# Moving two convolution taps from VectorE to TensorE in the last stage of a recurrent block, with a new VectorE order

## The chip, the cores and the metric

The kernel runs on one core of one Trainium2 chip. The metric is the device time of one execution in microseconds (us). Each time is the median of several executions. The profile is one of these executions, seen by the hardware profiler. All times inside it count from the start of its span.

Engine names: PE is TensorE (PEld its weight loads), DVE is VectorE, ACT is ScalarE, POOL is GpSimd, SP is SyncE.

## The reference, cut to what matters

There are 8 sequences of 512 tokens with 128 channels. Layer 0 is a causal attention multiplied by a gated top-2 mixture of experts. Layer 1, which the change touches, has a causal depthwise convolution with 7 taps, a gated recurrence and a gated feed-forward block. Everything is float32.

```python
h = rmsnorm(x, norm1_w)
local = causal_depthwise_conv(h, conv_w)           # sum over 7 taps j: h shifted by j, times conv_w[:, j]
decay = clip(sigmoid(h @ Wdecay + bdecay), 0.05, 0.95)
gate = sigmoid(h @ Wgate + bgate)
cumdecay = exp(cumsum(log(decay)))                 # a running product along the tokens
weighted_updates = gate * h / maximum(cumdecay_shifted, 1e-07)
state = cumsum(weighted_updates) * cumdecay * state_scale
mem = (h @ Wk) @ M.T @ Wmem * mem_scale
mixed = x + concat([local, state, mem]) @ Wc + bc
h2 = rmsnorm(mixed, norm2_w)
s = mixed + silu(h2 @ Wg) * (h2 @ Wup) @ Wdown
g = silu(tanh(x @ weight @ aux_weight1 @ aux_weight2 + bias))
out = x0 + s * g                                   # x is layernorm(x0)
```

The convolution is followed by a matrix, Wc. So a tap can be computed in either of two ways: as a scaled shift of h added into a tile (work per element), or inside a matmul whose weights are Wc with its rows scaled by that tap.

## The kernel before, in words

The program has four stages: the layer norm of all tokens; attention, sequence by sequence; the experts, one tile of 128 rows after the other (71 tiles); and layer 1, which the kernel's functions with the prefix `d_` compute. Layer 1 goes sequence by sequence, and one sequence b is one step (`d_step(b)`) on every engine. Channels lie on partitions and the 512 tokens of the sequence in the free dimension, so that most instructions there are 128x512. A 128x512 float32 matmul shows as two records ("x2") in the trace. Each engine runs its own list of steps written by hand, and semaphores join them. Steps 1 to 5 on DVE and ACT, and 1 to 6 on PE, are loops; step 0 and the last ones are written out.

The steps overlap. While PE works on the feed-forward block of sequence b, the engines prepare the gates, the running product, the convolution and the recurrence of b + 1, and the statistics of b + 2.

PE in step b, in order: `d_conv_end` (L898, adds the DVE part of the convolution, the tile LOC, into bank 4), `d_state` (L902, adds the state), `d_turn(b+1)` (L871 and L874, transposes), `d_back(b-1)` (L955, transposes the finished output), `d_ffn1` (L908), `d_squares` (L915), `d_gates(b+1)` (L887, L888), `d_roots` (L921), `d_conv(b+1)` (L894, the taps done by matmul, into bank 4), then the feed-forward block: `d_up` (L936 the gate half, L942 the up half) for four chunks c, and `d_down` (L947) for the same four, which runs one chunk behind.

DVE in step b: `d_mixed` (L1353), `d_add` (L1390), `d_meansq` (L1360), two `d_local` (L1367, one tap each into LOC), `d_h2_of` (L1373), `d_decay` (L1328), `d_cumulate` (L1332, the running product), then the four `d_gated` (L1380, each lets one `d_down` go) with these in between: the statistics of b + 2 (L1282, then L1287, then `d_radicands` L1293 and L1295), `d_floor` (L1340, lets POOL go on with the update), three more `d_local`, and `d_front3` (L1322, the normalised tile XN1 of b + 2). `d_scan` (L1347, the recurrence) and `d_sum` (L1386) end the step.

ACT squares (L1695), copies the turned tiles (L1656, L1663, L1670), computes the gates (L1677 to L1682) and the SiLU of each chunk (L1712), and at the end of a step scales the normalised tile of b + 2 for the next turn (L1688). POOL has the reciprocal roots (L557, L558 and L580, `pow` on 4 columns), additions and products (L545, L550, L566, L571) and the gated output OF (L576), which `d_back` waits for.

`LOCAL` is the number of taps outside the matmul: tap 0 on ACT (L1663), taps 1 to LOCAL - 1 on DVE. The scaled matrices for the others are TAPW. They are made once by ACT (L1567), between the softmax tiles of the first sequence.

Ahead of step 0 there is a prologue. PE runs bf16 matmuls on constants (`keep_warm`, L618) while DVE does the whole chain for sequence 0.

Of the kernel before, what the change touches and what calls it, by code (L numbers as in the profile page):

```python
# [22 lines left out]
ALU = mybir.AluOpType  # L23
# [5 lines left out]
TPS = SEQ // P  # L29
# [3 lines left out]
TAPS = 7  # L33
# [25 lines left out]


NB = NSEQ - 1
LOCAL = 6
COMBINE_AFTER = {2: 0, 3: 1, 6: 2, 7: 3}


# [11 lines left out]
def build(nc, t, out):  # L77
    ctx = ExitStack()
    with ctx:
# [361 lines left out]
        def _(pool):  # L441
# [110 lines left out]
            def scales(b):  # L552
                pool.wait_ge(d_vv, b + 1)
                if b >= 1:
                    pool.wait_ge(d_xn, b)
                    pool.wait_ge(d_hs, b)
                pool.tensor_tensor(R1, VLN, HALF[:, 0:TPS], ALU.pow).then_inc(d_r1, 1)  # L557
                link(pool.tensor_tensor(RRMS, VRMS, HALF[:, 0:TPS], ALU.pow))  # L558
                link(pool.tensor_tensor(R2, RRMS, VLN, ALU.mult))
                pool.wait_ge(d_r1, b + 1)  # L560
                pool.tensor_tensor(R2, R2, R1, ALU.mult).then_inc(d_r, 1)

            def update_gated(b):
# [48 lines left out]
        def _(pe):  # L612
# [274 lines left out]
                pe.matmul(B[bank][:], W3[:, 0, :], HP1[:, PAD:], start=True, stop=True)  # L887
                pe.matmul(B[bank + 1][:], W3[:, 1, :], HP1[:, PAD:], start=True, stop=True).then_inc(d_dg, 1)  # L888

            def d_conv(b):  # L890
                if not (isinstance(b, int) and b == 0):
                    pe.wait_ge(d_mix, b)
                for j in range(LOCAL, TAPS):
                    pe.matmul(B[4][:], TAPW[:, j - LOCAL, :], HP1[:, j:j + SEQ], start=(j == LOCAL), stop=False)  # L894

            def d_conv_end(b):
                pe.wait_ge(d_loc, (LOCAL - 1) * (b + 1))
                pe.matmul(B[4][:], W3[:, 2, :], LOC, start=False, stop=False).then_inc(d_taps, 1)  # L898

# [58 lines left out]
            def d_step(b, first=False, last=False):  # L958

                d_conv_end(b)  # L960
                d_state(b)
                if not last:
                    d_turn(b + 1)
                if not first:
                    d_back(b - 1)
                d_ffn1(b)
                d_squares(b)
                if not last:
                    d_gates(b + 1)
                d_roots(b)  # L970
                if not last:
                    d_conv(b + 1)
                d_up(b, 0)
                d_up(b, 1, last)
                d_down(b, 0)
                d_up(b, 2)
                d_down(b, 1)
                d_up(b, 3)
                d_down(b, 2)
                d_down(b, 3)  # L980
# [11 lines left out]
            d_turn(0)  # L992
            keep_warm(3, 2)
            d_gates(0)
            d_conv(0)
            keep_warm(3, 12)
            d_step(0, first=True)
            with pe.Fori(1, NSEQ - 1) as b:
# [6 lines left out]
        def _(dve):  # L1005
# [387 lines left out]
            def d_step(b, first=False, front=True, last=False):  # L1393
# [8 lines left out]
                if not last:  # L1402
                    d_decay(b + 1)
                    d_cumulate(b + 1)
                d_gated(b, 0)
                if front:
                    d_later_stats(b + 2)
                if not last:
                    d_floor(b + 1)
                if front:  # L1410
                    d_aggregate(b + 2)
                d_gated(b, 1)
                if front:
                    d_radicands(b + 2)
                if not last:
                    d_local(b + 1, 3)
                d_gated(b, 2)
                if not last:
                    d_local(b + 1, 4)
                if front:  # L1420
                    d_front3(b + 2)
                d_gated(b, 3)
                if not last:
                    d_local(b + 1, 5)
                    d_scan(b + 1)
                d_sum(b)

            dve.wait_ge(c_gelu, FC * SLOT_TILES)
# [9 lines left out]
            d_cumulate(0)  # L1438
            d_floor(0)
            d_first_update()  # L1440
            for j in range(3, LOCAL):
                d_local(0, j)
            d_scan(0)
            d_front3(1)
            d_step(0, first=True)
# [382 lines left out]
```

## Time and profile before

| what | us |
|---|---|
| median of 3 runs (575.05 to 577.47) | 575.14 |
| the profiled execution's own time | 575.05 |
| its span in the trace | 573.2 |
| PE busy over the span | 539.0 (94%) |
| DVE busy over the span | 384.2 (67%) |
| ACT busy over the span | 276.3 (48%) |
| POOL busy over the span | 258.0 (45%) |

Layer 1 takes the stretch from about 387 us to the end of the span. The stretch of its loop, 410 to 548 us, is the part to read closely. The timeline lists instructions in order of their start, merges a run of the same line, and gives in brackets how long the engine had been idle and who released it. A start less the start of the row above is the time that the engine truly needs for a piece of work, since the durations of matmuls overlap.

### The profile page before, as it was taken

The numbers are of one execution on the slowest core, as the hardware profiler recorded it, in microseconds if no ns is written. First come the engines' busy times: TensorE is split into PE (matmuls) and PEld (weight loads), VectorE is DVE, ScalarE is ACT, GpSimd is POOL, SyncE is SP. The second block draws the span as 40 slices with busy tenths as digits, with TensorE's granted clock in tenths as the row PEclk, the third lists the DMA queues.
The fourth block names the chain that finished last, engine by engine and source line by source line (L and its number), as shares of the span: only waits on it lengthen the run. The fifth ranks groups of instructions, "written<-read, shape, count | busy, mean of one in ns | idle before, by whom it ended". The sixth has DMA issues, their size and how long they took to land. (4 is left out here: it accounts for less than half of the span.)

```text
span 573.2 us, 13361 instructions
## 1 busy us (share of the span) xinstructions
PE 539.0 (94%) x3295; PEld 397.8 (69%) x3296; DVE 384.2 (67%) x1087; ACT 276.3 (48%) x790; POOL 258.0 (45%) x393
## 2 busy tenths in 40 slices
PE   9959899999989999999999999988899999999974
PEld 4735666666759999999999999963444554554441
DVE  6968777877764655555555555656588779778631
ACT  3513465465465545555454555474535644554320
POOL 4303554665622444444444444425256565664310
PEclk9978999999999999999999999999799999999988
DMA  9910533211116887888788878273000000000000
GB/s 285 398 61 20 178 118 132 81 65 55 42 28 182 235 232 237 235 240 238 235 234 233 232 237 239 83 215 88 2 0 20 18 18 0 18 18 5 15 18 18
DMA packets 46107, 71.77 MB, mean 125 GB/s; under 512 B 6256, under 2 KB 32016, under 8 KB 45824
## 3 DMA queue, kind: packets, MB, share of 16 engines
q1 hardware_dynamic: 31536, 57.82, 33.5%
q0 software_dynamic: 4320, 8.92, 4.7%
q10 hardware_dynamic: 10224, 4.73, 2.9%
q8 instruction: 10, 0.16, 0.1%
q14 instruction: 17, 0.14, 0.1%
HBM read 54.14 MB, written 15.74 MB: 122 GB/s over the span
## 5 line engine op out<-in xcount | busy, mean ns | idle before, releaser
L1223 DVE SCALAR_TENSOR_TENSOR AR<-bank,B1T,AR 128x128 f32<-128x128 f32 x284 | 80.5, 345 | 75.6 <-ACT AR L1605 75.4
L520 POOL DMA_INDIRECT rows_y<-YO,DST x71 | 69.8, 982 | 97.8 <-DVE YO L1207 94.9
L1605 ACT ACTIVATE AR<-bank,BGT 128x128 f32<-128x128 f32 x284 | 81.2, 368 | 57.4 <-PE bank L810 57.4
L476 POOL DMA_INDIRECT slots_x<-XR,SLOT x64 | 63.0, 984 | 50.8 <-DMA slots_x<-XR,SLOT 30.8
L827 PE MATMUL bank<-W2E,AR 128*128 x568 | 75.1, 275 | 0.5 <-DVE AR L1223 0.5
L810 PE MATMUL bank<-AR,WGE 128*128 128x128 f32 x568 | 75.1, 275 | 0.4 <-ACT AR L1598 0.4
L818 PE MATMUL bank<-AR,WGE 128*128 128x128 f32 x568 | 75.0, 275 | 0.0
L827 PEld LDWEIGHTS bank<-W2E,AR 128*128 128x128 f32 x568 | 69.1, 192 | 0.7 <-issue 0.7
L810 PEld LDWEIGHTS bank<-AR,WGE 128*128 128x128 f32 x568 | 69.0, 192 | 0.6 <-issue 0.6
L818 PEld LDWEIGHTS bank<-AR,WGE 128*128 128x128 f32 x568 | 69.1, 192 | 0.0
L1517 ACT ACTIVATE AR<-bank,AR 128x512 f32<-128x512 f32 (+1 forms) x64 | 33.9, 530 | 64.5 <-DVE AR L1146 64.5
L720 PE MATMUL bank<-AR 128*128 128x128 f32 x320 | 47.4, 280 | 0.9 <-ACT AR L1535 0.9
L1146 DVE TENSOR_REDUCE AR<-bank 128x1 f32<-128x512 f32 (+1 forms) x64 | 30.7, 483 | 22.9 <-PE bank L689 22.9
L687 PE MATMUL bank<-AR 128*128 128x128 f32 (+3 forms) x128 | 45.6, 440 | 0.0
L720 PEld LDWEIGHTS bank<-AR 128*128 128x128 f32 x320 | 41.7, 195 | 1.7 <-ACT AR L1526 1.6
L1712 ACT ACTIVATE W1E<-bank 128x512 f32<-128x512 f32 x32 | 19.1, 597 | 48.3 <-PE bank L936 48.3
L701 PEld LDWEIGHTS bank<-CST,AR 128*128 128x128 f32 x160 | 17.8, 141 | 35.2 <-ACT AR L1517 26.3
L1598 ACT ACTIVATE AR<-bank 128x128 f32<-128x128 f32 x71 | 19.6, 278 | 39.4 <-PE bank L802 39.4
L701 PE MATMUL bank<-CST,AR 128*128 128x128 f32 x160 | 29.8, 284 | 8.2 <-ACT AR L1517 8.1
L936 PE MATMUL bank<-WGE,WGT 128*128 128x512 f32 x64 | 34.4, 620 | 0.8 <-DVE WGE L1373 0.8
L947 PE MATMUL bank<-W1E,WDN 128*128 128x512 f32 x64 | 33.9, 614 | 0.7 <-DVE W1E L1380 0.2
L942 PE MATMUL bank<-WGE,WUP 128*128 128x512 f32 x64 | 33.6, 607 | 0.0
(191 smaller groups left out, 949.0 us busy)
## 6 DMA issues: line engine op xcount, KB each, us to landing
WGE<-in_wgu SPq DMA_DIRECT2D x71, 512.0 KB, 3.7
XG<-slots_x ACTq DMA_DIRECT2D x71, 65.0 KB, 3.2
slots_x<-W1E SPq DMA_DIRECT2D x7, 585.0 KB, 10.1
X<-in_x SPq DMA_DIRECT2D x8, 256.0 KB, 5.0
W2E<-in_w SPq DMA_DIRECT2D x1, 2048.0 KB, 8.5
XR<-rows_y SPq DMA_DIRECT2D x8, 256.0 KB, 4.8
XNT<-rows_y SPq DMA_DIRECT2D x8, 256.0 KB, 5.0
out<-X SPq DMA_DIRECT2D x8, 256.0 KB, 2.3
```

What stands on the lines that cost most here:

```text
L476: pool.indirect_dma_start(out=slots_x, out_offset=bass.IndirectOffsetOnAxis(ap=SLOT[:, k, n:n + 1], axis=0), in_=XR[:, n, :], in_offset=No ...
L520: pool.indirect_dma_start(out=rows_y, out_offset=bass.IndirectOffsetOnAxis(ap=DST[q][:, 0:1], axis=0), in_=YO[q % 2][:], in_offset=None).t ...
L687: pe.matmul(bank[:, 0:(i + 1) * P], QT[u][h][:, i * P:(i + 1) * P], QT[u][2][:, 0:(i + 1) * P], start=True, stop=False)
L701: mm = pe.transpose(B[4 + k % 2][:, j * P:(j + 1) * P], PR[k % 2][:, j * P:(j + 1) * P], ident)
L720: mm = pe.matmul(reg, PT[k % 2][:, j * P:(j + 1) * P], U[u][:, j, h * P:(h + 1) * P], start=(j == 0), stop=(j == i))
L810: mm = pe.matmul(B[1 + u][:, c * P:(c + 1) * P], WB[:, q, c * P:(c + 1) * P], XT[u], start=True, stop=True)
L818: mm = pe.matmul(B[3 + u][:, c * P:(c + 1) * P], WB[:, q, F + c * P:F + (c + 1) * P], XT[u], start=True, stop=True)
L827: mm = pe.matmul(B[5 + u][:, 0:P], HT[u][:, c, :], W2E[:, bass.ds(e, 1), c, :], start=(c == 0), stop=(c == FC - 1))
L936: pe.matmul(B[5 - 3 * (c % 2)][:], WGT[:, c * P:(c + 1) * P], H2, start=True, stop=True).then_inc(d_g, 1)
L947: mm = pe.matmul(B[7][:], WDN[:, c, :], UU[:, c, :], start=(c == 0), stop=(c == FC - 1))
L1223: s = dve.scalar_tensor_tensor(out=HT[u][:, c, :], in0=B[3 + u][:, c * P:(c + 1) * P], scalar=B1T[:, bass.ds(e, 1), c], in1=ZB[u][:, c, :] ...
L1605: act.activation(ZB[u][:, c, :], B[1 + u][:, c * P:(c + 1) * P], ACT.Gelu, bias=BGT[:, bass.ds(e, 1), c]).then_inc(c_gelu, 1)
```

## The change

`LOCAL` goes from 6 to 4. Taps 4 and 5 leave DVE and become matmuls beside tap 6. `d_conv` now takes a range of taps: taps 4 and 5 stand where tap 6 alone stood (after `d_roots`), and tap 6 moves to the front of `d_conv_end`, behind the last `d_down` of the step before. DVE loses two of its five `d_local` in each step, and the rest of its order changes: the statistics go in front of the first `d_gated`, `d_aggregate` and `d_radicands` in front of `d_floor`, and `d_front3` behind `d_scan`. POOL computes both reciprocal roots of a tile in one `pow` on 8 columns instead of two on 4. ACT makes three scaled matrices instead of one.

```diff
--- before.py
+++ after.py
@@ -59,7 +59,8 @@
 
 
 NB = NSEQ - 1
-LOCAL = 6
+LOCAL = 4
+CONV_PARTS = LOCAL + 1, LOCAL + 2
 COMBINE_AFTER = {2: 0, 3: 1, 6: 2, 7: 3}
 
 
@@ -554,10 +555,9 @@
                 if b >= 1:
                     pool.wait_ge(d_xn, b)
                     pool.wait_ge(d_hs, b)
-                pool.tensor_tensor(R1, VLN, HALF[:, 0:TPS], ALU.pow).then_inc(d_r1, 1)
-                link(pool.tensor_tensor(RRMS, VRMS, HALF[:, 0:TPS], ALU.pow))
+                pool.tensor_tensor(RV1, VV1, HALF[:, 0:2 * TPS], ALU.pow).then_inc(d_r1, 1)
+                pool.wait_ge(d_r1, b + 1)
                 link(pool.tensor_tensor(R2, RRMS, VLN, ALU.mult))
-                pool.wait_ge(d_r1, b + 1)
                 pool.tensor_tensor(R2, R2, R1, ALU.mult).then_inc(d_r, 1)
 
             def update_gated(b):
@@ -887,13 +887,14 @@
                 pe.matmul(B[bank][:], W3[:, 0, :], HP1[:, PAD:], start=True, stop=True)
                 pe.matmul(B[bank + 1][:], W3[:, 1, :], HP1[:, PAD:], start=True, stop=True).then_inc(d_dg, 1)
 
-            def d_conv(b):
-                if not (isinstance(b, int) and b == 0):
+            def d_conv(b, lo, hi):
+                if lo == LOCAL and not (isinstance(b, int) and b == 0):
                     pe.wait_ge(d_mix, b)
-                for j in range(LOCAL, TAPS):
+                for j in range(lo, hi):
                     pe.matmul(B[4][:], TAPW[:, j - LOCAL, :], HP1[:, j:j + SEQ], start=(j == LOCAL), stop=False)
 
             def d_conv_end(b):
+                d_conv(b, CONV_PARTS[1], TAPS)
                 pe.wait_ge(d_loc, (LOCAL - 1) * (b + 1))
                 pe.matmul(B[4][:], W3[:, 2, :], LOC, start=False, stop=False).then_inc(d_taps, 1)
 
@@ -969,7 +970,7 @@
                     d_gates(b + 1)
                 d_roots(b)
                 if not last:
-                    d_conv(b + 1)
+                    d_conv(b + 1, LOCAL, CONV_PARTS[1])
                 d_up(b, 0)
                 d_up(b, 1, last)
                 d_down(b, 0)
@@ -992,7 +993,7 @@
             d_turn(0)
             keep_warm(3, 2)
             d_gates(0)
-            d_conv(0)
+            d_conv(0, LOCAL, CONV_PARTS[1])
             keep_warm(3, 12)
             d_step(0, first=True)
             with pe.Fori(1, NSEQ - 1) as b:
@@ -1402,27 +1403,23 @@
                 if not last:
                     d_decay(b + 1)
                     d_cumulate(b + 1)
+                if front:
+                    d_later_stats(b + 2)
                 d_gated(b, 0)
                 if front:
-                    d_later_stats(b + 2)
+                    d_aggregate(b + 2)
+                    d_radicands(b + 2)
                 if not last:
                     d_floor(b + 1)
-                if front:
-                    d_aggregate(b + 2)
                 d_gated(b, 1)
-                if front:
-                    d_radicands(b + 2)
                 if not last:
                     d_local(b + 1, 3)
                 d_gated(b, 2)
+                d_gated(b, 3)
                 if not last:
-                    d_local(b + 1, 4)
+                    d_scan(b + 1)
                 if front:
                     d_front3(b + 2)
-                d_gated(b, 3)
-                if not last:
-                    d_local(b + 1, 5)
-                    d_scan(b + 1)
                 d_sum(b)
 
             dve.wait_ge(c_gelu, FC * SLOT_TILES)
@@ -1438,8 +1435,7 @@
             d_cumulate(0)
             d_floor(0)
             d_first_update()
-            for j in range(3, LOCAL):
-                d_local(0, j)
+            d_local(0, 3)
             d_scan(0)
             d_front3(1)
             d_step(0, first=True)
```

DVE, step 0, from the running product (writes W2E) to `d_front3`. The name WGE stands for the tiles DEC, GTE, STA, MIX and others, SPARE for LOC, CLP, the statistics and XN1, and the TENSOR_TENSOR into W1E is `d_gated`. Before:

```order
L1332 SCALAR_TENSOR_TENSOR W2E<-WGE,SPARE 128x512
L1380 TENSOR_TENSOR W1E<-bank6,W1E 128x512
L1282 BN_STATS SPARE<-X 128x6 x4
L1340 TENSOR_SCALAR SPARE<-W2E 128x512
L1287 BN_AGGR SPARE<-SPARE 128x2 x4
L1380 TENSOR_TENSOR W1E<-bank3,W1E 128x512
L1293 TENSOR_SCALAR SPARE<-SPARE 128x4
L1295 SCALAR_TENSOR_TENSOR SPARE<-SPARE 128x4
L1367 SCALAR_TENSOR_TENSOR SPARE<-W2E,VEC,SPARE 128x512
L1380 TENSOR_TENSOR W1E<-bank6,W1E 128x512
L1367 SCALAR_TENSOR_TENSOR SPARE<-W2E,VEC,SPARE 128x512
L1322 TENSOR_SCALAR SPARE<-X,SPARE 128x128 x4
```

The same place after the change (its line numbers are one higher):

```order
L1333 SCALAR_TENSOR_TENSOR W2E<-WGE,SPARE 128x512
L1283 BN_STATS SPARE<-X 128x6 x4
L1381 TENSOR_TENSOR W1E<-bank6,W1E 128x512
L1288 BN_AGGR SPARE<-SPARE 128x2 x4
L1294 TENSOR_SCALAR SPARE<-SPARE 128x4
L1296 SCALAR_TENSOR_TENSOR SPARE<-SPARE 128x4
L1341 TENSOR_SCALAR SPARE<-W2E 128x512
L1381 TENSOR_TENSOR W1E<-bank3,W1E 128x512
L1368 SCALAR_TENSOR_TENSOR SPARE<-W2E,VEC,SPARE 128x512
L1381 TENSOR_TENSOR W1E<-bank6,W1E 128x512
L1381 TENSOR_TENSOR W1E<-bank3,W1E 128x512
L1348 SCALAR_TENSOR_TENSOR WGE<-WGE 128x512
```

The first `d_gated` now stands behind the four BN_STATS, and the scan (L1348) directly behind the last one, with `d_front3` after it.

PE, from the end of step 0 into the loop's first instructions (L948 and L947 are `d_down`, bank 4 is the convolution). Before:

```order
L942 MATMUL bank3<-WGE,WUP 128x512
L947 MATMUL bank7<-W1E,WDN 128x512 x2
L998 UNCONDITIONAL_BRANCH
L998 ISA
L898 MATMUL bank4<-SPARE,W3 128x512
L902 MATMUL bank4<-WGE,WST 128x512
```

After:

```order
L943 MATMUL bank3<-WGE,WUP 128x512
L948 MATMUL bank7<-W1E,WDN 128x512 x2
L999 UNCONDITIONAL_BRANCH
L894 MATMUL bank4<-W2E,TAPW 128x512
L898 ISA
L899 MATMUL bank4<-SPARE,W3 128x512
L903 MATMUL bank4<-WGE,WST 128x512
```

Tap 6 now stands between the last `d_down` and the matmul that takes LOC.

## Rows read from the trace of the kernel before

**Rows 1.** Windows: stretch, us, busy PE, PEld, DVE, ACT, POOL, PEclk, DMA share, GB/s.
```profile
469.60:489.30 19.70, 19.57 (x65) 9.53 (x64) 16.02 (x33) 9.96 (x20) 12.08 (x11) 1.00 0.04 13
...
404.00:410.30 6.30, 6.30 (x14) 3.39 (x15) 2.73 (x6) 3.04 (x7) 0.00 (x0) 0.55 0.01 3
554.00:555.00 1.00, 1.00 (x3) 0.48 (x2) 0.00 (x0) 0.60 (x1) 0.00 (x0) 0.50 0.00 0
```

**Rows 2.** Timeline of PE, one step: start, us, engine, line, operation, tiles, shape.
```profile
463.31 2.27 PE L947 MATMUL bank<-W1E,WDN 128*128 128x512 f32 x4
465.42 1.02 PE L898 MATMUL bank<-SPARE,W 128*128 128x512 f32 x2
...
468.26 0.65 PE L955 MATMUL bank<-CST,SPARE 128*128 128x128 f32 x4
...
469.61 0.95 PE L915 MATMUL bank<-MEAN,WGE 128*128 128x1 f32 x8
...
473.11 1.02 PE L894 MATMUL bank<-W2E,TAPW 128*128 128x512 f32 x2
474.12 1.12 PE L936 MATMUL bank<-WGE,WGT 128*128 128x512 f32 x2
...
477.80 1.12 PE L947 MATMUL bank<-W1E,WDN 128*128 128x512 f32 x2
...
483.05 2.26 PE L947 MATMUL bank<-W1E,WDN 128*128 128x512 f32 x4
```

**Rows 3.** Timeline of DVE in the same step, from the first d_gated on.
```profile
477.08 0.66 DVE L1380 TENSOR_TENSOR W1E<-bank,W1E 128x512 f32<-128x512 f32 x1
477.66 0.86 DVE L1282 BATCH_NORM_STATS2 SPARE<-X 128x6 f32 x4
478.55 0.43 DVE L1340 TENSOR_SCALAR SPARE<-W2E 128x512 f32<-128x512 f32 x1
...
482.43 1.11 DVE L1322 TENSOR_SCALAR SPARE<-X,SPARE 128x128 f32 x4
483.45 0.68 DVE L1380 TENSOR_TENSOR W1E<-bank,W1E 128x512 f32<-128x512 f32 x1
```

**Rows 4.** Timeline of POOL and ACT: first pow, gated output, scaling for the turn.
```profile
387.74 1.04 POOL L557 TENSOR_TENSOR SPARE<-SPARE,HALF 128x4 f32<-128x4 f32 x1 [4.84 <-DVE SPARE L1295]
...
466.85 1.27 POOL L576 TENSOR_TENSOR SPARE<-SPARE,WGE 128x512 f32<-128x512 f32 x1 [2.65 <-DVE SPARE L1386]
...
484.02 1.28 ACT L1688 ACTIVATE SPARE<-SPARE 128x128 f32<-128x128 f32 x4 [1.04 <-POOL SPARE L561]
```

**Rows 5.** Timeline of DVE and PE around the end of step 6.
```profile
542.25 2.07 PE L947 MATMUL bank<-W1E,WDN 128*128 128x512 f32 x4
...
542.46 0.69 DVE L1380 TENSOR_TENSOR W1E<-bank,W1E 128x512 f32<-128x512 f32 x1 [1.23 <-PE bank L942]
...
544.16 1.02 PE L898 MATMUL bank<-SPARE,W 128*128 128x512 f32 x2
...
546.92 0.66 PE L955 MATMUL bank<-CST,SPARE 128*128 128x128 f32 x4 [0.80 <-POOL SPARE L576]
```

**Rows 6.** Timeline of DVE, PE and ACT in the prologue and at step 0's start.
```profile
396.83 2.75 PE L618 MATMUL bank<-ONB 128*128 128x512 bf16 x12
...
401.38 2.46 DVE L1367 SCALAR_TENSOR_TENSOR SPARE<-W2E,VEC,SPARE 128x512 f32<-128x512 f32 x3
403.76 1.22 DVE L1347 TENSOR_TENSOR_SCAN WGE<-WGE 128x512 f32<-128x512 f32 x1
...
403.89 2.08 PE L898 MATMUL bank<-SPARE,W 128*128 128x512 f32 x2 [4.31 <-DVE SPARE L1367]
...
406.01 1.27 ACT L1688 ACTIVATE SPARE<-SPARE 128x128 f32<-128x128 f32 x4 [7.54 <-DVE SPARE L1322]
407.47 1.06 PE L871 MATMUL bank<-CST,SPARE 128*128 128x128 f32 x4
...
410.31 0.95 PE L915 MATMUL bank<-MEAN,WGE 128*128 128x1 f32 x8
```

## What was predicted before the changed kernel ran

> **What bounds the kernel now.** I read the windows first, then the timeline of PE for one step of the layer-1 loop, then DVE's for the same step, then the prologue. In the loop PE is busy for 19.57 us of 19.70, at a granted clock of 1.00, so at its upper level of 2.4 GHz; DVE is busy for 16.02 [rows 1]. The start of the down matmuls of two successive steps (463.31 and 483.05) gives the period, 19.74 us [rows 2]. So PE is the bound, but that share hides small stalls, since durations of matmuls overlap. What one 128x512 float32 matmul needs is read from start to start: between the first d_down of a step (477.80) and the third (483.05) stand six of them in 5.25. The first started late, and its record of 1.12 instead of 1.02 shows what that adds, 0.10 (its weights aren't loaded ahead). So one takes (5.25 - 0.10) / 6 = 0.86 [rows 2].
>
> The stalls of a period, in that unit: the last two d_down take 2.11 instead of 1.72, 0.39 lost, because PE waits for the fourth d_gated. From d_conv_end to d_back 2.84 instead of 2.58 (two matmuls and two turns of 0.43), 0.26 lost, to the scan and to OF, which POOL ends at 468.12 against a start of 468.26 [rows 2, 4]. 0.15 behind tap 6 for the tile H2, and 0.10 for the late start. The four up matmuls from 474.12 take 0.10 + 4 x 0.86 = 3.54, the first d_down starts 3.68 after, 0.06 behind the end of the first d_gated: 0.14, and 0.10 for its own late start [rows 2, 3]. Together 1.14, so the work of PE alone is 19.74 - 1.14 = 18.60.
>
> **The change part by part.** *Two more matmuls per step.* 2 x 0.86 = 1.72 us of PE. 18.60 + 1.72 = 20.32 is the least that a period can now be, 0.58 above the old one, and all of it lies on PE's own path. What DVE saves (two L1367 of about 0.75 each, by the three in 2.46 of rows 6) lies beside it.
>
> The rest is what the waits become. I count from the start of d_squares, old 469.61, as 0. *Down to the first d_down.* The taps 4 and 5 end 0.71 later than tap 6 did (0.86, less the 0.15 wait for H2 that they now cover). The up matmuls then start at 474.83, and PE could start the first d_down 4 x 0.86 later, at 478.27. But on DVE the running product ends at its old time, because the gates, which it hangs on, come before the taps; and the statistics now stand ahead of the first d_gated. They take 478.55 - 477.66 = 0.89, so this d_gated starts at 477.97, ends at 478.63, and d_down starts at 478.69: 0.89 later than before, and 0.42 of this is PE waiting [rows 2, 3]. The added tap of this place is thus covered, and what counts is DVE's order.
>
> *To the last d_down.* d_aggregate, d_radicands, d_floor, d_gated and one d_local follow within about 2.5 us, before the third up matmul is out, so the next two d_gated meet PE's pace. The six matmuls up to the third d_down are as long as before (5.25). The fourth d_gated no longer stands behind a tap and d_front3. Step 6, which has no d_front3, shows the wait that is left: 544.16 - 542.25 = 1.91 for the two d_down instead of 2.11, so -0.20 [rows 2, 5].
>
> *Tap 6 in d_conv_end.* +0.86. It covers what came late there: the scan starts 0.60 after the start of the fourth d_gated and takes 1.22 [rows 6], which is over before tap 6 and LOC's matmul are. d_sum now stands behind d_front3 (1.02 from start to start, 483.45 - 482.43). From the last d_gated's start: scan 0.60, d_front3 1.73 (the next instruction starts about 0.1 before a record ends), d_sum 2.75, its end 3.41 (0.66 as for a d_gated), and 0.07 and 1.27 for POOL: OF at 4.75 [rows 3, 4]. PE's d_back is due 5.15 after that start: 1.70 of d_down are left (1.91, less the 0.21 between the starts at 542.25 and 542.46), then tap 6, LOC and the state with 0.86 each, and the turn with 0.87 [rows 5]. So the whole stall of 0.26 goes. *d_front3's other customer* is ACT, which scales the tile in 1.28, and then PE turns it: 1.73 + 1.11 + 0.05 + 1.28 + 0.06 = 4.23 after that start, while PE is due at 4.28. Before, it had 1.6 us in hand. This one is tight; I book 0.03 for it.
>
> Sum of a period: 0.89 - 0.20 + 0.86 - 0.26 + 0.03 = **1.32**, so 21.06. There are six such periods (steps 0 to 5): **+7.9**. From step 6 to step 7 there are no statistics, so the first d_gated has no extra wait: two taps 1.72, less 0.25 at H2, less what PE waited for OF. That was 546.92 - 544.16 less two matmuls, 1.04, of which I leave 0.08; the new tap fills the rest and nothing but the scan stands ahead of d_sum [rows 5]: 1.72 - 0.25 - 0.96 = **+0.5**.
>
> *Prologue.* DVE does one tap instead of three before the scan, each 0.855 from start to start, so everything behind is 1.71 earlier. PE waited 4.31 us, and then ran at a clock of 0.50 to 0.55, its lower level of 1.2 GHz, into step 0 [rows 1, 6]. From the turn to d_squares it took 410.31 - 407.47 = 2.84 where at the upper level two turns of 0.43 and one matmul take 1.73. PE now has two taps more to do in the hole, one before and one after keep_warm, and the hole shrinks to about 1.0 us in front of LOC and 1.4 in front of the turn, which still hangs on d_front3 and ACT (406.01 + 1.27, less 1.71). If the clock stays up, step 0's d_squares comes 1.71 + 1.11 = 2.8 earlier. If it falls at a later point, the dense work of step 0 runs low for a while; 6.3 us low were seen, so at most 3.1 lost. The row nearest in kind is step 7: there the clock fell to 0.50 by 554 after several short holes, the first of 0.80, between short work [rows 1, 5]. I take a fall that costs 1.1: **-1.7** (-2.8 to +0.2).
>
> *The joint pow.* Not in the trace. One pow on 4 columns takes 1.04, so two take 2.08 [rows 4]. On 8 columns it lies between 1.04 and 2.1. In the loop POOL has over 3 us in hand, since R1 is wanted only behind the scan. In the prologue d_front3(0) waits for it and PE has about 0.2 in hand: 0 to +0.4, I take **+0.1**. *Two more scaled matrices* on ACT, 0.4 each beside the softmax of the first sequence, where ACT mostly waits: 0 to +0.8, I take **+0.1**.
>
> Total: 7.9 + 0.5 - 1.7 + 0.1 + 0.1 = **+6.9** on the profiled execution's own 575.05, so 581.9; the median of the runs, 575.14, is the same to 0.1.
>
> **What the Trainium skill would say.** Its page "Trainium Kernel Development and Optimization", section Best Practices, says that the distance to the roofline is not to be judged by how busy matmul makes PE look; that would leave room on PE for the taps. The trace agrees only in part: beside 19.57 of 19.70 busy there are 1.14 us per period of room, less than the taps. The page "TensorE: Matmul & The Clock Gate", section "Wait — 56ns, not 53.3ns?", gives N / 2.4 GHz + 2.5 ns for a matmul in a row, 0.22 us for 512 columns. The float32 rows here show four times as much, and the rows decide. By that price the sum would be smaller by what the rival of the cheap taps says.
>
> **The rivals.**
> *The stalls dissolve.* Not slower, and the one mechanism is PE's own rate: if the gates' chain on DVE ends earlier (POOL out of its way), the first d_down doesn't wait, and each period is 20.3. It needs that all waits of 1.14 go. Then 6 x 0.58 + 0.5 = 4.0, less 2.8 in the prologue and up to 1.7 if the low clock of step 7 goes as well (an estimate: some 3 us at half rate around the row of 554): 574.6 [rows 1]. It decides from a period under 20.35. Against it: the running product's start is not moved by anything. 0.08.
> *In between.* Period 20.7, since part of the 0.42 is hidden, and the clock stays up in the prologue: 6 x 0.95 + 0.5 - 2.8 + 0.2 = +3.6, 578.7. 0.20.
> *DVE's tail becomes the bound.* d_front3, ACT's scaling and the turn have nothing in hand; 0.5 us more there (a port shared with POOL, a wait that I don't see) is on the path six times: +3, so 585. 0.15.
> *Cheap taps.* The 128x512 bf16 matmuls of keep_warm run at 2.75 / 12 = 0.23 each [rows 6]. If a tap cost that, the one in d_conv_end would cost 0.63 less in each of 7 steps, 4.4 in all: 577.5. Against it stands tap 6, which as a float32 matmul of the same shape costs 0.86 here. 0.02. The figure of the Trainium skill's page "TensorE: Matmul & The Clock Gate" would have it so.
> *My sum,* 581.9, from 579.8 to 584: 0.55.
>
> **How the numbers follow.** Predicted is the likeliest, 581.9. The range leaves out the first rival and the far half of the slow one: 577 to 585. A measurement of this kernel tells 0.5% (2.9 us) from no change. Faster by over 0.5% (below 572.3) needs more than the whole first rival: 0.03. Within: most of that rival and half of the cheap taps, some of the one in between: 0.12. Slower: 0.85.
>
> **What would show it.** Right: a period of about 21.0 in the new trace, the first d_down of a step starting 0.06 behind the end of the first d_gated with PE idle before it, no wait at d_back, and ACT's scaling ending within 0.2 of the turn. PE idle before LOC's matmul in the prologue near 1 us. Wrong: a period under 20.5, or a d_gated that ends well before its d_down is due; or a turn that waits for ACT by more than 0.1.

## The result, and the profile after

The changed kernel took 585.31 us in the median (583.39 to 586.44, 4 runs), beside 576.31 for the kernel before on the same chip (575.05 to 578.09, 4 runs): a ratio of 1.0157, 95% interval 1.0131 to 1.0183. It is slower, as forecast, and 0.3 us above the range; the forecast was 581.9. Of the 3.4 us between the two, 1.2 are not the sum's: it was built on 575.05 to 575.14 for the kernel before, whose median came out at 576.31 with a fourth run. The change in the medians is +9.0 where +6.9 was forecast. The profiled execution took 584.18, 9.1 more than that of before.

The page's line of busy times of the changed kernel:

```profile
PE 546.8 (94%) x3327; PEld 401.7 (69%) x3328; DVE 377.0 (65%) x1071; ACT 276.7 (48%) x792; POOL 255.1 (44%) x385
```

PE has 7.7 us more to do (546.76 against 539.05 before rounding), DVE 7.2 less, and the kernel is 9.1 longer. The shares alone don't say where.

The loop first. This is PE's timeline of the changed kernel over one period; its columns are those of [rows 2].

```profile
451.66 0.95 PE L916 MATMUL bank<-MEAN,WGE 128*128 128x1 f32 x8
...
455.51 1.88 PE L894 MATMUL bank<-W2E,TAPW 128*128 128x512 f32 x4
457.24 1.02 PE L937 MATMUL bank<-WGE,WGT 128*128 128x512 f32 x2
...
461.10 1.13 PE L948 MATMUL bank<-W1E,WDN 128*128 128x512 f32 x2 [0.27 <-DVE W1E L1381]
...
466.35 2.07 PE L948 MATMUL bank<-W1E,WDN 128*128 128x512 f32 x4
468.26 1.02 PE L894 MATMUL bank<-W2E,TAPW 128*128 128x512 f32 x2
469.12 1.02 PE L899 MATMUL bank<-SPARE,W 128*128 128x512 f32 x2
469.98 1.02 PE L903 MATMUL bank<-WGE,WST 128*128 128x512 f32 x2
470.84 0.60 PE L871 MATMUL bank<-CST,SPARE 128*128 128x128 f32 x4
471.27 0.60 PE L874 MATMUL bank<-CST,SPARE 128*128 128x128 f32 x4
471.71 0.60 PE L956 MATMUL bank<-CST,SPARE 128*128 128x128 f32 x4
...
473.01 0.95 PE L916 MATMUL bank<-MEAN,WGE 128*128 128x1 f32 x8
```

From d_squares to d_squares it is 473.01 - 451.66 = 21.35, where before it was 19.74. The only wait that the rows name is in front of the first d_down, 9.44 behind d_squares; before it was 477.80 - 469.61 = 8.19 [rows 2], so 1.25 of the 1.61 are there. From d_conv_end on every row starts when the one above lets it: the stall at d_back is gone and the turn doesn't wait for ACT.

What DVE and POOL did ahead of that d_down (the rows of DVE answer to [rows 3], those of POOL are of the same step):

```profile
457.38 2.00 DVE L1333 TENSOR_TENSOR_SCAN W2E<-WGE,SPARE 128x512 f32<-128x512 f32 x1
459.30 0.84 DVE L1283 BATCH_NORM_STATS2 SPARE<-X 128x6 f32 x4
460.35 0.69 DVE L1381 TENSOR_TENSOR W1E<-bank,W1E 128x512 f32<-128x512 f32 x1 [0.21 <-DVE SPARE L1283]
```
```profile
452.89 1.58 POOL L580 TENSOR_TENSOR SPARE<-SPARE,HALF 128x4 f32<-128x4 f32 x1 [1.67 <-DVE SPARE L1361]
...
463.38 2.10 POOL L558 TENSOR_TENSOR SPARE<-SPARE,HALF 128x8 f32<-128x8 f32 x1
```

The statistics cost 460.35 - 459.30 = 1.05 in front of the d_gated, not 0.89, because DVE waits 0.21 for their own result to land. The d_gated doesn't read that result. The wait is the program's: `d_later_stats` ends with a wait for its own last BN_STATS, and it holds whatever comes next. In the kernel before `d_floor` stood behind the same wait and started 0.89 after the statistics [rows 3]; why it was held less isn't known. No run moves the wait down to `d_aggregate`, the first instruction that needs it. And the statistics start 7.64 behind d_squares, the place where the first d_gated stood at 7.47 before. POOL's pow for the RMS roots took 1.58 where it took 1.02 in steps 1 to 5 before.

The prologue, rows of PE, POOL and DVE of the changed kernel in order of time, and under them two rows of windows (columns as in [rows 1]); they answer to [rows 4, 6]:

```profile
387.81 5.34 PE L618 MATMUL bank<-ONB 128*128 128x512 bf16 x24
...
388.51 1.68 POOL L558 TENSOR_TENSOR SPARE<-SPARE,HALF 128x8 f32<-128x8 f32 x1 [4.93 <-DVE SPARE L1296]
...
390.29 2.06 DVE L1323 TENSOR_SCALAR SPARE<-X,SPARE 128x128 f32<-128x128 f32 x4 [1.28 <-POOL SPARE L558]
...
390.70 1.32 POOL L546 TENSOR_TENSOR XR<-XR,SA 128x512 f32<-128x512 f32 x1
...
393.98 0.63 PE L871 MATMUL bank<-CST,SPARE 128*128 128x128 f32 x4 [0.82 <-ACT SPARE L1684]
...
403.96 1.12 PE L899 MATMUL bank<-SPARE,W 128*128 128x512 f32 x2 [0.88 <-DVE SPARE L1368]
...
407.41 0.66 PE L871 MATMUL bank<-CST,SPARE 128*128 128x128 f32 x4 [1.19 <-ACT SPARE L1684]
...
409.20 0.95 PE L916 MATMUL bank<-MEAN,WGE 128*128 128x1 f32 x8
```
```profile
392.00:404.00 12.00, 9.81 (x39) 4.36 (x37) 8.18 (x22) 5.36 (x11) 4.18 (x5) 1.00 0.03 8
404.00:412.00 8.00, 6.80 (x27) 3.38 (x27) 4.38 (x9) 4.79 (x10) 1.57 (x2) 1.00 0.00 0
```

PE's hole in front of LOC's matmul shrank from 4.31 to 0.88, and the granted clock stayed at 1.00, its upper level, where it had been 0.55 over 6.3 us [rows 1]. From the gates of sequence 0 to its d_squares it took 13.24 instead of 16.13. Against that, the first turn starts 6.17 behind the first warm-up matmul instead of 5.18. The rows of before for the start of `d_front3` (L1322) there:

```profile
388.77 1.01 POOL L558 TENSOR_TENSOR SPARE<-SPARE,HALF 128x4 f32<-128x4 f32 x1
388.89 1.11 DVE L1322 TENSOR_SCALAR SPARE<-X,SPARE 128x128 f32<-128x128 f32 x4 [0.65 <-POOL SPARE L557]
```

| where | before | after | difference | forecast |
|---|---|---|---|---|
| start to the first warm-up matmul | 387.04 | 387.81 | +0.77 | +0.1 |
| from there to the first turn | 5.18 | 6.17 | +0.99 | +0.1 |
| from there to step 0's d_squares | 18.09 | 15.22 | -2.87 | -1.7 |
| six periods | 118.52 | 127.84 | +9.32 | +7.9 |
| step 6 to step 7 | 19.44 | 20.25 | +0.81 | +0.5 |
| rest | 24.93 | 25.01 | +0.08 | 0 |
| span | 573.2 | 582.3 | +9.1 | +6.9 |

The rest, from step 7's d_squares to the end, is equal in these two executions but not in all: over all the traces it lies between 23.4 and 26.4, at a granted clock of 0.90 to 0.75, and for the changed kernel itself it was 25.01 once and 26.4 once. The start of layer 1 moves too. So the experiments are judged by their periods first; a median is moved by both ends as well.

### The profile page after: what moved, and what is told of

Read it like the earlier page. It is cut to its first block and busy times, and to the rows that moved or that the text cites. A ratio compares the mean times of both kernels' runs of the same rounds, so it can differ in the third digit from the quotient of the medians.

```text
span 582.3 us, 13385 instructions
## 1 busy us (share of the span) xinstructions
PE 546.8 (94%) x3327; PEld 401.7 (69%) x3328; DVE 377.0 (65%) x1071; ACT 276.7 (48%) x792; POOL 255.1 (44%) x385
## 5 line engine op out<-in xcount | busy, mean ns | idle before, releaser
L1381 DVE TENSOR_TENSOR W1E<-bank,W1E 128x512 f32<-128x512 f32 x32 | 22.1, 690 | 25.9 <-PE bank L943 24.7
L948 PE MATMUL bank<-W1E,WDN 128*128 128x512 f32 x64 | 33.5, 615 | 1.5 <-DVE W1E L1381 1.3
```

Source lines behind the costliest of these rows:

```text
L948: mm = pe.matmul(B[7][:], WDN[:, c, :], UU[:, c, :], start=(c == 0), stop=(c == FC - 1))
```

## The experiments

Periods are from one d_squares to the next inside the loop. A ratio stands against the kernel before on the same chip, with its 95% interval.

### The taps alone, and the rest alone

The taps alone: in the kernel before, LOCAL is 4 and the convolution is split as in the change. DVE's order and both pows stay.

```diff
-LOCAL = 6
+LOCAL = 4
+CONV_PARTS = LOCAL + 1, LOCAL + 2
...
+                d_conv(b, CONV_PARTS[1], TAPS)
                 pe.wait_ge(d_loc, (LOCAL - 1) * (b + 1))
```

> The kernel before with only the move of taps 4 and 5 to PE (tap 6 in d_conv_end, DVE simply loses its two last d_local); DVE's order and the two pow as before. Theory A (the new order of DVE sets the first d_down, the taps are partly covered): the first d_down is free of the statistics, so PE meets it on time at 8.7 to 8.9 us after the start of d_squares and the period is 20.5 to 20.8, prologue 2.9 shorter, so about 578 to 579, some 6 us under the changed kernel. Theory B (the two matmuls of 0.86 are the whole price, the order is incidental): period 21.3 as in the changed kernel, 583 to 585.

Measured: 580.28, ratio 1.0065 (1.0041 to 1.0088), a period of 20.46.

```profile
448.64 0.95 PE L917 MATMUL bank<-MEAN,WGE 128*128 128x1 f32 x8
...
456.44 1.02 PE L944 MATMUL bank<-WGE,WUP 128*128 128x512 f32 x2
457.30 1.02 PE L949 MATMUL bank<-W1E,WDN 128*128 128x512 f32 x2
```
```profile
456.11 0.66 DVE L1382 TENSOR_TENSOR W1E<-bank,W1E 128x512 f32<-128x512 f32 x1
456.69 0.85 DVE L1284 BATCH_NORM_STATS2 SPARE<-X 128x6 f32 x4
```

The first d_down starts 0.86 behind the row above it, so it waits for nothing: its d_gated was over at 456.77. The two matmuls, together 1.72, cost 0.72, since of the 1.14 of stalls only 0.14 is left.

The rest alone: the change's order and joint pow, with six taps outside the matmul as before.

```diff
-LOCAL = 4
-CONV_PARTS = LOCAL + 1, LOCAL + 2
+LOCAL = 6
+CONV_PARTS = TAPS, TAPS
...
                 d_gated(b, 2)
+                if not last:
+                    d_local(b + 1, 4)
                 d_gated(b, 3)
                 if not last:
+                    d_local(b + 1, 5)
                     d_scan(b + 1)
```

> The changed kernel with LOCAL back at 6: the new order of DVE and the joint pow, but all taps where they were. Theory A: d_gated behind the statistics makes the first d_down 0.9 to 1.2 late, and d_front3 behind the scan now makes the turn wait for ACT, since no tap 6 covers it: period about 21.5, prologue 1.0 longer for the pow, 585 to 588, slower than the changed kernel. Theory B: PE has no more work than before, period 19.8 to 20.0, about 577.

Measured: 589.77, ratio 1.0223 (1.0176 to 1.027), a period of 21.81, so slower than the whole change.

```profile
464.76 1.12 PE L948 MATMUL bank<-W1E,WDN 128*128 128x512 f32 x2 [1.06 <-DVE W1E L1381]
...
475.07 0.66 PE L871 MATMUL bank<-CST,SPARE 128*128 128x128 f32 x4 [1.19 <-ACT SPARE L1688]
```

PE waits twice, for the first d_gated and at the turn for ACT. The order and the joint pow cost 2.07 a period without the taps. The first d_down is 9.27 behind d_squares here and 9.26 in the kernel below with two taps more on PE and two pows. So the added tap ahead of it lies wholly in that wait. Tap 6 lies in the wait at the turn, as the experiment on it shows; here that wait is longer also because DVE still has a `d_local` ahead of the scan.

### Parts of DVE's order

The changed kernel with DVE's old order at the head of a step (first d_gated, statistics, floor, aggregate, second d_gated, radicands); the new tail and the joint pow stay.

```diff
-                if front:
-                    d_later_stats(b + 2)
                 d_gated(b, 0)
                 if front:
+                    d_later_stats(b + 2)
+                if not last:
+                    d_floor(b + 1)
+                if front:
                     d_aggregate(b + 2)
-                    d_radicands(b + 2)
-                if not last:
-                    d_floor(b + 1)
                 d_gated(b, 1)
+                if front:
+                    d_radicands(b + 2)
```

> The changed kernel (two more taps on PE, joint pow, the fourth d_gated, the scan and d_front3 in the new order), but at the head of a step DVE's order is that of the kernel before: first d_gated, statistics, d_floor, d_aggregate, second d_gated, d_radicands. Theory 1 (all that the order costs comes from the statistics ahead of the first d_gated): a period of 20.45 to 20.55, as in the kernel with the taps alone (20.46); its time is above that kernel's only by the joint pow in the prologue, 1.0: 578.6 profiled, a median near 581. Theory 2 (the new tail, with d_front3 behind the scan and in front of d_sum, costs PE time too, at d_back or at the turn): a period of 20.7 or more, a median of 582.5 or more.

Measured: 582.13, ratio 1.0089 (1.0066 to 1.0112), a period of 20.46, 578.63 profiled. The period is that of the taps alone, so the new tail costs nothing once tap 6 lies over it, and all of the order's price is in its head. That the profiled time meets the 578.6 expected is partly luck: against the kernel with the taps alone this execution started layer 1 1.67 later, and its end after step 7's d_squares was 1.7 shorter.

Half of the head: the first d_gated stands in front of the statistics again, but d_radicands stays in front of the second d_gated.

```diff
+                d_gated(b, 0)
                 if front:
                     d_later_stats(b + 2)
-                d_gated(b, 0)
+                if not last:
+                    d_floor(b + 1)
                 if front:
                     d_aggregate(b + 2)
                     d_radicands(b + 2)
-                if not last:
-                    d_floor(b + 1)
                 d_gated(b, 1)
```

> The changed kernel with the first d_gated of a step back in front of the statistics, and d_floor behind them in front of d_aggregate. Theory A: the first d_down starts when PE is ready, 8.9 after d_squares instead of 9.44, and its late start of 0.10 goes: period about 20.7, six times 0.6 less, about 3.7 us faster than the changed kernel. Theory B: no gain, 0 to 0.5 us.

Measured: 584.25, ratio 1.0132 (1.0087 to 1.0178), a period of 21.02. The first d_down is on time; the second is not. DVE, PE and POOL of this kernel:

```profile
460.55 1.04 DVE L1294 TENSOR_SCALAR SPARE<-SPARE 128x4 f32<-128x4 f32 x1
...
461.80 0.69 DVE L1381 TENSOR_TENSOR W1E<-bank,W1E 128x512 f32<-128x512 f32 x1
```
```profile
459.51 1.02 PE L948 MATMUL bank<-W1E,WDN 128*128 128x512 f32 x2
...
462.55 1.13 PE L948 MATMUL bank<-W1E,WDN 128*128 128x512 f32 x2 [0.30 <-DVE W1E L1381]
```
```profile
460.31 1.26 POOL L571 TENSOR_TENSOR WGE<-WGE,SPARE 128x512 f32<-128x512 f32 x1 [2.98 <-DVE SPARE L1341]
```

The first instruction of d_radicands, on four columns, takes 1.04 instead of 0.17 and ends at 461.59, 0.02 behind POOL's product (461.57). It stood still beside that product, which `d_floor` had just let go, and the second d_gated stood behind it. With d_radicands put back behind the second d_gated, as in the kernel above, the period is 20.46.

The Trainium skill, page "SBUF — State Buffer", section "SBUF: two separate sides", describes the port that GpSimd and VectorE share as a lock held for a whole instruction, with the other engine fully blocked. On VectorE's side it names instructions with two inputs in SBUF or in a 2-port mode. The trace agrees: the held instruction ends with POOL's product. Its kind (`tensor_scalar`) takes 0.43 for 128x512 [rows 3] where the d_gated, with the same columns, takes 0.66, which fits such a mode but doesn't show it.

### The joint pow

The changed kernel with two pows.

```diff
-                pool.tensor_tensor(RV1, VV1, HALF[:, 0:2 * TPS], ALU.pow).then_inc(d_r1, 1)
-                pool.wait_ge(d_r1, b + 1)
+                pool.tensor_tensor(R1, VLN, HALF[:, 0:TPS], ALU.pow).then_inc(d_r1, 1)
+                link(pool.tensor_tensor(RRMS, VRMS, HALF[:, 0:TPS], ALU.pow))
                 link(pool.tensor_tensor(R2, RRMS, VLN, ALU.mult))
+                pool.wait_ge(d_r1, b + 1)
```

> The changed kernel with two pow on 4 columns in place of one on 8. Theory A: only the prologue gains, since the normalised tile of sequence 0 starts 0.6 earlier and doesn't meet POOL's product at the port; PE's first turn comes about 1.0 us earlier, the period stays 21.35: about 1 us faster than the changed kernel. Rival (POOL's longer pow is behind the slower period too): period 21.1 or less, 2 to 3 us faster.

Measured: 582.37, ratio 1.0107 (1.0053 to 1.0161). The first turn starts 5.18 behind the first warm-up matmul again, so the 0.99 there is the joint pow's. The kernel with the joint pow alone, below, shows the same from the other side (6.19). The period is 21.17, not 21.35, which neither theory had (one kept 21.35, the other went to 21.1 or less). In this trace the RMS pow takes 1.02.

The joint pow alone, in the kernel before (the edit above, the other way round).

> The kernel before with one edit of the change: the two pows of 4 columns become one of 8 columns. Theory 1 (it costs only in the prologue, where d_front3 of sequence 0 waits for it and then runs beside POOL's product; in the loop POOL has time in hand): the turn of sequence 0 starts 6.1 to 6.2 us after the first warm-up matmul instead of 5.2, the periods stay at 19.73 to 19.75, the kernel is 0.8 to 1.1 us slower than the kernel before: a ratio of 1.0014 to 1.002. Theory 2 (in the loop the longer pow moves POOL's later work and with it DVE's, through the port they share): a period of 19.8 or more, 1.4 us or more slower in all.

Measured: 588.18 beside 586.07 for the kernel before, ratio 1.0052 (1.0014 to 1.0089), a period of 20.17 instead of 19.74. The chip of this run is slower ahead of layer 1: the two kernels traced on it started its first warm-up matmul 8.0 and 5.7 us later than their like on the other chips. The period of before, 19.74, is from another chip, so the comparison rests on the places inside a step, which the rows show. Six times 0.43 and 1.0 in the prologue make 3.6, inside the interval (0.8 to 5.2 us). The first theory is right on the prologue (6.1 to 6.2 foreseen, 6.19 measured) and fails on the loop, where it saw no price; the second foresaw one, by POOL's later work, but it comes by d_front3. DVE, then POOL and PE:

```profile
491.18 0.74 DVE L1366 SCALAR_TENSOR_TENSOR SPARE<-W2E,VEC,SPARE 128x512 f32<-128x512 f32 x1
492.26 1.11 DVE L1321 TENSOR_SCALAR SPARE<-X,SPARE 128x128 f32 x4 [0.34 <-issue]
493.29 0.68 DVE L1379 TENSOR_TENSOR W1E<-bank,W1E 128x512 f32<-128x512 f32 x1
```
```profile
490.04 2.12 POOL L557 TENSOR_TENSOR SPARE<-SPARE,HALF 128x8 f32<-128x8 f32 x1 [0.30 <-DVE SPARE L1294]
```
```profile
494.03 1.13 PE L946 MATMUL bank<-W1E,WDN 128*128 128x512 f32 x2 [0.55 <-DVE W1E L1379]
```

In the kernel before, the first pow of two was out 1.49 after its start. Here the joint one is out after 2.12, at 492.16, and d_front3 starts 0.10 behind that, 13.25 behind d_squares instead of 12.82. POOL's row of before for the pow:

```profile
480.63 1.49 POOL L557 TENSOR_TENSOR SPARE<-SPARE,HALF 128x4 f32<-128x4 f32 x1 [0.30 <-DVE SPARE L1295]
```

d_front3 (L1321) waits for this pow in the program, and in the old order the fourth d_gated and its d_down stand behind d_front3. A joint pow of 1.65, as in the kernel with the first d_gated in front, would have been out at 491.69, before DVE was through with the tap ahead of d_front3 (491.92). So the price hangs on the pow taking 2.12 here. In this trace a `d_local` started 0.13 ahead of the pow, and in the one with 1.65 it started 0.54 behind it. That is what a port shared by the two engines would do, but no run separates it. In the new tail d_front3 comes after the fourth d_gated and the scan: there the joint pow costs nothing in the loop (20.46 with it and the old head, 20.46 with two pows in the kernel of the taps alone).

### The long RMS pow

The changed kernel, but DVE starts the first tap of the next sequence only when POOL has finished that pow.

```diff
+                    dve.wait_ge(d_rs, b + 1)
```

> The changed kernel with one wait added: DVE starts the first d_local of the next sequence only when POOL has finished the pow of the RMS roots, so that no DVE instruction with two inputs in SBUF runs beside that pow. In the changed kernel the pow takes 1.58 beside them, alone it takes 1.02, and POOL's products and the whole chain up to the running product come 0.17 later. Theory 1 (the shared port lengthens the pow, and that is 0.17 of the period): the pow is back at 1.02, the first d_gated starts 0.1 to 0.2 earlier from the start of d_squares, a period of 21.15 to 21.25, a median of 584 to 584.7. Theory 2 (the chain on DVE is set by DVE's own work, and the pow's end is not on it; the added wait only pushes DVE back): a period of 21.35 or more, a median of 585.3 or more.

Measured: 588.54, ratio 1.0206 (1.0181 to 1.0232), a period of 22.05. DVE and POOL:

```profile
454.43 3.46 DVE L1368 SCALAR_TENSOR_TENSOR SPARE<-W2E,VEC,SPARE 128x512 f32<-128x512 f32 x2 [1.32 <-POOL SPARE L580]
```
```profile
453.20 1.02 POOL L580 TENSOR_TENSOR SPARE<-SPARE,HALF 128x4 f32<-128x4 f32 x1 [1.68 <-DVE SPARE L1361]
...
455.75 1.60 POOL L551 TENSOR_TENSOR X<-X,XR 128x512 f32<-128x512 f32 x1
```

The pow is back at 1.02, and at 1.02 and 1.01 in steps 0 and 6, where it had been 1.47 and 1.46: VectorE beside it can lengthen it. But the two taps take 3.46 instead of 1.54, since they now run beside POOL's product and addition (L546 and L551). The wait costs far more than it saves; the period is where the second theory had it, 21.35 or more, and the first theory is right only on the pow.

The changed kernel once more, unchanged.

> The changed kernel once more, unchanged, for one look. What is open: the pow of the RMS roots took 1.58 in its trace and 1.02 in the traces of kernels that differ little from it, at the same start relative to DVE's instructions. Theory 1 (the length belongs to this kernel's order): again 1.58, and a period of 21.35. Theory 2 (it falls one way or the other from execution to execution): 1.02 and a period of 21.17 to 21.2. The start of the first warm-up matmul, 387.81 in the first trace against 387.04 of the kernel before, is expected anywhere between 386.7 and 389.

Measured, on the slower chip: 590.35 in a single run, beside 586.07 for the kernel before; a period of 21.17, and for the pow:

```profile
458.44 1.02 POOL L580 TENSOR_TENSOR SPARE<-SPARE,HALF 128x4 f32<-128x4 f32 x1 [1.67 <-DVE SPARE L1361]
```

So the program doesn't fix the 1.58: one trace of this kernel has it in steps 1 to 5, the other in none, and with it go 0.18 of a period. Without it the period is 21.17, the same as with two pows. What decides which length comes isn't known (the execution and the chip both differ); DVE's tap starts 0.04 to 0.05 ahead of the pow in either case. Two traces don't tell which is the usual one. The medians 585.31 and, with two pows, 582.37 lie further apart than the 1.0 of the prologue, so it may be the longer one.

### Tap 6

The changed kernel with all three taps ahead of the up matmuls.

```diff
-CONV_PARTS = LOCAL + 1, LOCAL + 2
+CONV_PARTS = TAPS, TAPS
```

> The changed kernel with one line different: all three taps (4, 5, 6) stand ahead of the up matmuls, and d_conv_end holds LOC's matmul alone. The number of matmuls is unchanged. Theory 1: in d_conv_end tap 6 stands in a place where nothing else of PE could run, because d_front3, ACT's scaling of the tile and then PE's turn follow the fourth d_gated on a path of 4.2 to 4.3 us; taken away there, 0.86 of PE's work becomes 0.8 of waiting ahead of the turn (and up to 0.3 ahead of d_back). Ahead of the up matmuls it fills 0.27 of waiting at the first d_down and the rest, 0.6, is added: a period of 21.3 to 21.9 where the changed kernel has 21.35, a median of 585 to 589. Theory 2: the turn follows with PE, tap 6 costs its 0.86 where it stands, and moved to the place where PE waits for the first d_gated it costs less: a period of 20.9 to 21.1, a median of 582 to 583.5. The rows that tell: what PE waits for ahead of the turn in a step of the loop.

Measured: 587.25, ratio 1.0186 (1.0157 to 1.0214), a period of 21.28. The RMS pow is at 1.02 here, so it stands against 21.17.

```profile
470.52 1.02 PE L903 MATMUL bank<-WGE,WST 128*128 128x512 f32 x2
472.14 0.66 PE L871 MATMUL bank<-CST,SPARE 128*128 128x128 f32 x4 [0.61 <-ACT SPARE L1684]
```

Without tap 6 in d_conv_end PE waits for ACT at the turn instead: the next start is 1.62 behind L903's, not 0.86, so 0.76 of the tap's 0.86 is given back as waiting. The first d_down has no wait any more, as 0.86 was added ahead of it. The first theory is right on the mechanism (its period began at 21.3, its median of 585 to 589 was met), and the tap is better placed where the change has it, by 0.11 a period.

### The prologue's gain without the rest

The kernel before with its loop left alone; for sequence 0 only, taps 4 to 6 are matmuls of PE (the scaled matrices are then three, `WEIGHTED = 4`, and the loop goes on using the last of them).

```diff
+            def d_first_conv(lo, hi):
+                for j in range(lo, hi):
+                    pe.matmul(B[4][:], TAPW[:, j - WEIGHTED, :], HP1[:, j:j + SEQ], start=(j == WEIGHTED), stop=False)
...
-            d_conv(0)
+            d_first_conv(WEIGHTED, TAPS - 1)
             keep_warm(3, 12)
+            d_first_conv(TAPS - 1, TAPS)
...
-            for j in range(3, LOCAL):
+            for j in range(3, WEIGHTED):
                 d_local(0, j)
```

> The kernel before, whose loop is left as it was (one tap on PE, five on DVE, the old order, two pows), but for sequence 0 alone the taps 4, 5 and 6 are matmuls of PE, one ahead of and one behind the warm-up matmuls as in the changed kernel; ACT scales three matrices for it. Theory 1: the change's gain in the prologue is a thing by itself: DVE's scan of sequence 0 comes 1.71 earlier and PE's hole is so short that the clock stays at its upper level, so the time from the gates of sequence 0 to its d_squares falls from 16.13 to 13.24, and the periods stay at 19.74: about 572 profiled, a median 2.5 to 3.3 us below the kernel before, a ratio of 0.994 to 0.9957. Theory 2: the gain hangs on the rest of the change (the shorter wait in front of step 0 is paid back where DVE's work of step 0 is late, as in the first period of the changed kernel, which was 0.24 shorter than the others): 1 us or less is left, a ratio of 0.998 or more.

Measured: 573.66 beside 576.93, ratio 0.9943 (0.9923 to 0.9963), 572.11 profiled, periods of 19.70 to 19.71. The windows of its prologue and step 0:

```profile
387.00:407.00 20.00, 17.43 (x72) 8.20 (x72) 13.09 (x38) 8.72 (x19) 7.36 (x10) 1.00 0.25 60
407.00:427.00 20.00, 19.82 (x66) 9.52 (x65) 15.38 (x32) 9.96 (x20) 12.01 (x11) 1.00 0.00 0
```

The clock never falls, d_squares of step 0 is at 407.52 against 410.31, and nothing is paid back. The earlier scan and the clock come together here; no run has one without the other. This kernel is faster than both.

## Why the prediction missed, step by step

- **PE's own work: right.** 18.60 + 1.72 = 20.32 was called the least of a period. The taps alone gave 20.46, so the unit of 0.86 and the list of stalls held within 0.14.
- **Down to the first d_down, the term of 0.89: mis-sized, and the main miss.** The mechanism was right (statistics ahead of the first d_gated, PE waiting in front of d_down), and d_down does start 0.06 behind that d_gated's end. The size was 1.25 in the profiled execution, where the first d_down is 9.44 behind d_squares instead of the 9.08 worked out, and 1.07 with the shorter pow (9.26, in the kernel with two pows). Two things were left out. The four instructions of the statistics were priced by the start of the row that had followed them, 0.89. But the row that follows now is held until they have landed: 1.05. And the premise that "the running product ends at its old time" failed by 0.17 in this execution, where the RMS pow took 1.58. The first of these is 1.0 us over six periods, the second 0.9, over the five with the long pow. The steps further down came out 0.07 a period better than worked out, 0.4 in all, and 0.1 came back in the first period (+1.28 against the old one).
- **To the last d_down (-0.20), no wait at d_back (-0.26), the turn (+0.03), tap 6 (+0.86): right.** 466.35 to 468.26 is 1.91, as worked out. From d_conv_end to d_squares it is 4.75 where these terms give 4.82. The tight turn held; the experiment on tap 6 shows that only the tap holds it.
- **Step 6 to 7, +0.5: measured +0.81.** With OF no longer waited for, the next late thing is ACT's square of the mixed tile (L1691), which my count of this place didn't have; PE waits 0.28 for it:

```profile
557.29 1.05 PE L916 MATMUL bank<-MEAN,WGE 128*128 128x1 f32 x8 [0.28 <-ACT WGE L1691]
```
- **The prologue, -1.7: measured -2.87.** The clock stayed up. I had taken a fall that costs 1.1, by a likeness to step 7; the best case of the range was the true one. (By its own numbers, 3.1 lost against 2.8 won, the other bound is +0.3 and not +0.2; nothing hangs on it.)
- **The joint pow, 0 to +0.4 and taken as +0.1: measured +0.99, outside its bounds.** Its length was inside them (1.68 on 8 columns, so the first result is out 0.64 later than with 1.04). But d_front3, started that much later, now ran beside POOL's product (L546, 390.70 to 392.02) and took 2.06 instead of 1.11. Shifting an instruction brought it beside another one, and I had priced only the shift.
- **Ahead of layer 1, +0.1: +0.77 in the profiled execution.** Nothing points to the change: with the same two more matrices, the kernels above started their warm-up anywhere from 386.74 to 388.90, on chips where the kernel before took 576 to 577. What goes with a late start is PE's clock between 38 and 42 us. In the changed kernel's trace PE ran at a clock of 0.82 between 38 and 42 us, against 1.00 before:

```profile
38.00:42.00 4.00, 3.40 (x12) 1.38 (x10) 2.34 (x8) 1.79 (x5) 0.00 (x0) 0.82 0.00 0
```

  Of the ten traces that are not from the slower chip, four have 0.79 to 0.87 there, and these start the warm-up at 387.81 to 388.90; the other six have 1.00 and start at 386.74 to 387.41. One of the four makes a single scaled matrix, like the kernel before. The cause of the lower clock isn't known.

The loop's miss (+1.4), step 6 (+0.3), the pow (+0.9) and the start (+0.7) make 3.3 too little, the prologue gives 1.2 back: about the 2.2 between +6.9 and +9.1. The median of 585.31 adds the 1.2 of the kernel before. The prediction's rival of 585 had its 0.5 per step in DVE's tail and the turn; the time came out there, but by DVE's head, so that rival was not right, only near.

## What to carry to other kernels

Work moved off an engine that isn't the bound gives time only where somebody waits for that engine, and only as much as that wait. In the loop all stalls of PE together were 1.14 a period, less than the 1.72 that the taps cost it. In the prologue its wait for DVE was 4.31, and taking the change only there is the faster kernel. When an instruction is put in front of one that the bound waits for, look for the waits that come along with it, and price it until its result has landed. And of every instruction that shifts, ask which one of the other engine on the shared port it now runs beside.

## What the runs showed of the hardware

- A VectorE `tensor_scalar` beside a GpSimd product on 128x512 is held, in both sizes seen: 1.04 instead of 0.17 on 128x4, 2.06 instead of 1.11 on four times 128x128. Beside a GpSimd `pow` on 128x4 the same four took 1.11.
- A GpSimd `pow` costs by its columns: 1.04 on 4 columns and 1.68 on 8 in the same place of the prologue. In the loop, on 8 columns, it took 2.09 to 2.13 in most kernels and 1.65 in the one with the first d_gated in front.
- The same `pow` at the same place beside the same VectorE instruction took 1.58 in steps 1 to 5 of one execution of this kernel and 1.02 in those of another. Why stays open.
- In the prologue all three traces with a hole of PE of 4.31 us have a granted clock of 0.55 to 0.73 over the 6.3 us before step 0's d_squares; all nine with holes of 0.88 and 1.19 have 1.00.
